# The output stores of every second pair of tiles, sent as 120 channels and 8 channels

## Chip, core and metric

The kernel runs on one core of a Trainium2 chip. The metric is the device time of one execution in microseconds; the kernel before takes 663.94 us (median of three runs, 661.92 to 664.46).

## What is computed

The input is one image of 256 channels and 96x96 points in float32. Two layers are added to it, one after the other. Only the second one matters here (b is 1, there are K = 4 heads):

```python
proj    = einsum('bchw,oc->bohw', gn(x), Wc) + bc
flows   = einsum('bchw,koc->kbohw', gn(x), Woff) + boff      # 4 offsets (x, y) for each point
weights = softmax(einsum('bchw,kc->bkhw', gn(x), Wwt) + bwt, axis=1)
feats   = bilinear sample of proj at (point + flow), zero outside the image, for each head
x       = x + einsum('kbohw,bkhw->bohw', feats, weights)
```

So each point of the output is a weighted sum of 16 vectors of 256 channels (4 heads x 4 corners), read at places that depend on the data.

## The kernel before

The image stays in SBUF as `xs` (128 channels on the partitions, two blocks `CB` of them, 9216 points). The points are cut into NT = 72 tiles of 128 points, and two tiles are a pair: 36 pairs.

The first 250 us or so load the image (SP queue), compute the first layer and write the result, turned so that one point is one row of 1 KB, into a `table` in HBM, each row twice: a row of the table holds the 256 channels of a point and of the point below it. Two neighbouring rows, 4 KB, hold all four corners of one sample.

The last 400 us or so are the second layer. For each tile and each head, GpSimd (POOL in the profile, line 948) issues one indirect DMA: 128 rows of 4 KB, 512 KB, one to a partition, into one of 16 places (`RING` = 4 tiles x 4 heads). The place can be refilled when both VectorE and TensorE have read it, so GpSimd waits on `added` and `used` before each issue. There are 72 x 4 = 288 of these gathers. Their destinations are called `v` and `stage` in the profile.

VectorE (DVE) sums 9 or 10 of the 16 corners of most tiles (lines 1155 and 1158, the first one of a tile at line 1155); TensorE (PE) sums the others as matmuls with diagonal matrices that ScalarE (ACT) makes (line 1528). VectorE joins the two sums (line 1165), TensorE turns the joined sum (line 1541) and multiplies it by the projection weights (lines 1553 and 1555), and VectorE adds the result of a pair to `xs` (line 1172), which raises `out_ready`. For the last pair the turn, the product and the addition go tile by tile (lines 1573, 1588, 1590 and 1203).

All stores of the output are on the SP queue. It waits for `out_ready` and issues one store for a pair: 128 partitions x 2 blocks x 256 points of float32, 256 KB in pieces of 1 KB (line 903), `LAST` = 35 times, and then one store of 128 KB for each of the last two tiles (line 908). SP has nothing else to do in the second layer. Nothing waits for a store but the end of the program, where SP waits for `written`.

A transfer is carried by the 16 DMA engines of the core together, and each engine that has done its part adds one to the transfer's semaphore; a wait for a multiple of 16 waits for all of them. The two kinds of transfer have different queues in the profile: q0 (software_dynamic) is what GpSimd issues, q1 (hardware_dynamic) what SP issues. q8 and q14 (instruction) are fetches of the program itself.

```python
for p in range(LAST):
    sp.wait_ge(out_ready, p + 1)
    sp.dma_start(out_c[:, :, p * 2 * P:(p + 1) * 2 * P], xs[:, :, p * 2 * P:(p + 1) * 2 * P]) \
        .then_inc(written, 16)
```

Of the kernel before, what the change touches and what calls it, by code (L numbers as in the profile page):

```python
# [34 lines left out]
P = 128  # L35
# [106 lines left out]
def build(nc, x, WqT, bq, WvT, bv, WpT, bp, out):  # L142
# [3 lines left out]
    out_c = out.rearrange("a (t p) h w -> p (a t) (h w)", p=P)  # L146
# [3 lines left out]
    with ExitStack() as ctx:  # L150
        def sb(name, shape, dt=F32):
            return ctx.enter_context(nc.sbuf_tensor(name, shape, dt))

        def sem(name):
            return ctx.enter_context(nc.semaphore(name))

        ps = ctx.enter_context(nc.psum_tensor("ps", [P, 8, CHUNK], F32))
        xs = sb("xs", [P, CB, HW])
# [22 lines left out]
        def column(name, n=1):  # L181
            if name not in col:
                col[name] = (sum(w for _, w in col.values()), n)
            a, w = col[name]
            return small[:, a:a + w]
# [13 lines left out]
        with ExitStack() as c0:  # L199
# [449 lines left out]
            with ExitStack() as c3:  # L649
# [16 lines left out]
                def chunk_of(n):  # L666
                    return n % 3 * ROUNDS + n // 3
# [60 lines left out]
                def sb3(name, shape, dt=F32):  # L728
                    return c3.enter_context(nc.sbuf_tensor(name, shape, dt))
# [6 lines left out]
                PAIRS = NT // 2  # L736
# [47 lines left out]
                share = sb3("share", [P, MOST])  # L784
                wy = sb3("wy", [P, 2, MOST, HEADS])

                DIAGS = 4
                assert max(NP) < 8

# [6 lines left out]
                RING = 4  # L796
                assert len(places) == DIAGS + RING * HEADS

                def place_of(t, k):
                    return DIAGS + t % RING * HEADS + k  # L800

# [9 lines left out]

                diag = [[a[:, n * P:(n + 1) * P] for n in range(max(NP))] for a in places[:DIAGS]]
                diag_sum = [a[:, 7 * P:8 * P] for a in places[:DIAGS]]

# [24 lines left out]
                weights_ready = sem("weights_ready")  # L839
                landed = {i: sem(f"landed{i}") for i in range(DIAGS, len(places))}  # L840
                added = sem("added")
# [8 lines left out]
                written = sem("written")  # L850
# [15 lines left out]
                def last_of_head(t, k):  # L866
                    return max(n for n, (head, _) in enumerate(ON_DVE[kind(t)]) if head == k)
# [5 lines left out]
                def used_by(t, k):  # L873

                    return t * HEADS + k + 1

                with nc.Block(no_gpsimd_drain=True) as block:
                    @block.sync
                    def _(sp):
                        sp.wait_ge(parts_ready, 2)  # L880
                        sp.dma_start(bias_row[:, :], bp.rearrange("(a n) -> a n", a=1).broadcast_to([P, NPROJ])).then_inc(grid_landed, 16)
                        sp.dma_start(grid[:, :, :], k_["grid"]).then_inc(grid_landed, 16)

                        sp.wait_ge(zeros_ready, 1)
                        sp.dma_start(table[0:W, 0:C], zeros).then_inc(edges_stored, 16)
                        sp.dma_start(table[HW:HW + W, C:2 * C], zeros).then_inc(edges_stored, 16)

                        def store(n):
                            u = n % SLOTS
                            for h in range(2):  # L890
                                sp.wait_ge(stage_ready, 2 * n + h + 1)
                                r = chunk_of(n) * CHUNK + h * 2 * P
                                sp.dma_start(table[r + W:r + W + 2 * P, 0:C].rearrange("(a p) c -> p a c", p=P),
                                             stage[u][h]).then_inc(stored[u], 16)
                                sp.dma_start(table[r:r + 2 * P, C:2 * C].rearrange("(a p) c -> p a c", p=P),
                                             stage[u][h]).then_inc(stored[u], 16)

                        for n in range(NCH):
                            store(n)

                        for p in range(LAST):
                            sp.wait_ge(out_ready, p + 1)
                            sp.dma_start(out_c[:, :, p * 2 * P:(p + 1) * 2 * P], xs[:, :, p * 2 * P:(p + 1) * 2 * P]) \
                                .then_inc(written, 16)
                        for i in range(2):
                            sp.wait_ge(out_ready, LAST + 1 + i)
                            here = slice((NT - 2 + i) * P, (NT - 1 + i) * P)
                            sp.dma_start(out_c[:, :, here], xs[:, :, here]).then_inc(written, 16)
                        sp.wait_ge(written, 16 * (PAIRS + 1))

                    @block.gpsimd
                    def _(pool):
# [294 lines left out]
                    def _(act):  # L1207
# [91 lines left out]
                        def diags(t):  # L1299
                            if t in FIRST:  # L1300
                                act.wait_ge(weights_ready, GROUP_OF[t] + 1)
                            if t >= DIAGS:
                                act.wait_ge(used, used_by(t - DIAGS, HEADS - 1))
# [376 lines left out]
```

## Time and profile before

| what | value |
|---|---|
| three runs, median (lowest to highest) | 663.94 us (661.92 to 664.46) |
| the profiled execution, its own time | 663.88 us |
| its span, first to last instruction | 661.9 us |
| mean granted clock of TensorE | 0.964 |
| busy: PE, DVE, POOL, ACT | 580.0, 550.2, 364.5, 362.3 us |
| moved by the DMA engines | 197.04 MB |

The span is what the profile's rows are placed in: a row at 640 us is 640 us after the first instruction. The device time of the same execution is 2.0 us more than the span. Packets are the pieces that DMA engines move; a queue's share is the time that its packets took, as a share of 16 engines over the stretch asked for. One engine that is busy all the time is therefore 1/16 or 6.25%.

### The profile page before, as it was taken

The page shows a single profiled execution, that of the slowest core. Times are in us where ns is not written, and L with a number is a line of the kernel's source. Part 1 is how long each engine was busy: PE and PEld are TensorE (multiplying, and loading weights), DVE is VectorE, ACT ScalarE, POOL GpSimd, SP SyncE. Part 2 cuts the span into 40 slices and gives each one's busy share as a digit, 9 for nine tenths or more (in the row PEclk, how much of TensorE's full clock was granted, in tenths as well). Part 3 has the DMA queues.
Part 4 walks back from the last instruction along what each step waited for, and adds up shares of the span by engine and source line. Part 5 has one row for each costly group of instructions (what it writes and reads, how often), then busy time and mean ns, then how long its engine had stood idle before and what let it go on. Part 6 is the DMA issues. An engine that isn't in the chain of part 4 may idle for free.

```text
span 661.9 us, 10746 instructions
## 1 busy us (share of the span) xinstructions
PE 580.0 (88%) x2992; PEld 457.2 (69%) x2992; DVE 550.2 (83%) x1316; ACT 362.3 (55%) x892; POOL 364.5 (55%) x385
## 2 busy tenths in 40 slices
PE   0589989999999789989969998989999899897987
PEld 0233477577888578878858996868777777675776
DVE  7899776458999878799888988978898879887886
ACT  0288876778888546165363556363645454535331
POOL 0040197115555447777776776776577566766620
PEclk9989999999999956799998999999999999999999
DMA  9910000214777778999999999999999999999982
GB/s 351 412 43 0 0 1 1 74 34 123 220 213 214 254 255 295 409 408 411 409 409 411 409 412 411 412 410 412 411 411 410 412 408 411 411 412 410 412 315 71
DMA packets 77367, 197.04 MB, mean 298 GB/s; under 512 B 7338, under 2 KB 36813, under 8 KB 77197
## 3 DMA queue, kind: packets, MB, share of 16 engines
q0 software_dynamic: 43488, 154.55, 59.4%
q1 hardware_dynamic: 33836, 42.03, 18.1%
q8 instruction: 14, 0.23, 0.2%
q14 instruction: 29, 0.23, 0.1%
HBM read 168.05 MB, written 28.51 MB: 297 GB/s over the span
## 4 chain that ended last, share of the span: by engine, by line
DMA 35%; PE 16%; issue 5%; DVE 4%; POOL 3%; ACT 1%; POOLq 0%; DVEq 0%
DMA v<-table,index 32%; PE ps L1528 9%; PE ps L1553 3%; DMA stage<-table,index 3%; DVE ps L1158 2%; POOL v L948 2%; PE ps L1555 2%; PE ps L1478 1%; POOL stage L948 1%; PE ps L1541 0%; DVE ps L1155 0%; ACT v L1305 0%; PE ps L1588 0%; POOL xs L935 0%; DVE wvs L1158 0%
## 5 line engine op out<-in xcount | busy, mean ns | idle before, releaser
L948 POOL DMA_INDIRECT v<-table,index x252 | 236.2, 937 | 106.6 <-DVE ps L1158 39.9
L1528 PE MATMUL ps<-v 128*128 128x256 f32 x786 | 205.8, 399 | 36.5 <-DMA v<-table,index 27.0
L1158 DVE SCALAR_TENSOR_TENSOR ps<-v,weights,ps 128x256 f32<-128x256 f32 x489 | 214.5, 483 | 1.5
L1528 PEld LDWEIGHTS ps<-v 128*128 128x128 f32 x786 | 142.3, 196 | 80.0 <-DMA v<-table,index 53.9
L1305 ACT ACTIVATE v<-ident,weights 128x128 f32<-128x128 f32 x464 | 139.4, 388 | 5.4 <-DVE wsum L1111 2.8
L935 POOL TENSOR_TENSOR xs<-xs,v 128x512 f32<-128x512 f32 x36 | 45.1, 1273 | 46.1 <-DVE v L1005 46.1
L1397 PE MATMUL ps<-wq,s_ring 128*128 128x256 f32 x288 | 68.1, 380 | 1.0 <-ACT ps L1241 0.9
L1318 ACT COPY pick_mask<-ps 128x512 f32<-128x512 f32 x18 | 10.5, 585 | 106.0 <-PE ps L1541 106.0
L1155 DVE TENSOR_SCALAR ps<-v,weights 128x256 f32<-128x256 f32 x72 | 34.9, 485 | 39.0 <-DMA v<-table,index 38.8
L1318 ACT COPY sample<-ps 128x512 f32<-128x512 f32 x17 | 9.9, 585 | 97.3 <-PE ps L1541 97.3
L1397 PEld LDWEIGHTS ps<-wq,s_ring 128*128 128x128 f32 x288 | 53.9, 191 | 9.4 <-issue 2.9
L559 PE MATMUL ps<-xs,wvs 128*128 (+1 forms) x104 | 49.9, 640 | 5.7 <-ACT v L494 3.4
L488 ACT ACTIVATE a_ring<-xs,small 128x768 f32<-128x768 f32 (+1 forms) x48 | 49.0, 1025 | 10.2 <-POOL t_ring L475 5.3
L475 POOL TENSOR_SCALAR t_ring<-a_ring,small 128x768 f32<-128x768 f32 x24 | 32.0, 1342 | 37.1 <-DVEq L416 34.9
L1555 PEld LDWEIGHTS ps<-v,bias 128*128 128x128 f32 x280 | 42.3, 191 | 3.6
L948 POOL DMA_INDIRECT stage<-table,index x36 | 33.7, 937 | 18.2 <-DVE ps L1158 10.9
L559 PEld LDWEIGHTS ps<-xs,wvs 128*128 128x128 f32 x104 | 20.4, 204 | 33.6 <-issue 25.9
L1555 PE MATMUL ps<-v,bias 128*128 128x128 f32 x280 | 42.5, 275 | 0.0
L1553 PE MATMUL ps<-pick_mask,wps 128*128 128x256 f32 x144 | 37.0, 380 | 0.0
L1528 PE MATMUL ps<-stage,v 128*128 128x256 f32 x142 | 34.6, 384 | 1.1 <-DMA stage<-table,index 0.9
L1553 PE MATMUL ps<-sample,wps 128*128 128x256 f32 x136 | 35.1, 381 | 0.0
L976 DVE TENSOR_REDUCE row_max<-ps 128x16 f32<-128x512 f32 x36 | 24.7, 687 | 10.0 <-PE ps L1397 9.0
(172 smaller groups left out, 926.8 us busy)
## 6 DMA issues: line engine op xcount, KB each, us to landing
table<-stage SPq DMA_DIRECT2D x72, 256.0 KB, 3.1
out_dram<-xs SPq DMA_DIRECT2D x35, 256.0 KB
xs<-in_x_dram SPq DMA_DIRECT2D x11, 768.0 KB, 11.3
v<-table,index POOLq DMA_INDIRECT x252, 16.0
early<-const_syn POOLq DMA_DIRECT2D x18, 192.0 KB, 3.6
ana<-const_ana SPq DMA_DIRECT2D x1, 2304.0 KB, 20.1
stage<-table,index POOLq DMA_INDIRECT x36, 15.7
xs<-in_x_dram SPq DMA_DIRECT2D x1, 512.0 KB, 14.8
```

The lines of the kernel that those rows point to most:

```text
L475: nc.gpsimd.tensor_scalar(t_ring[u][:, :], a_ring[u][:, :], column("less_mn")[:, t:t + 1], column("sc")[:, t:t + 1], ALU.add, ALU.mult).th ...
L488: S.activation(a_ring[u][:, :], xs[:, t, ds(j * (2 * QCH) + u * QCH, QCH)], ACT.Abs, scale=column("rstd")[:, t:t + 1], bias=column("nmr")[ ...
L559: m = T.matmul(ps[:, bank, :], wvs[:, kb, ob * P:(ob + 1) * P], xs[:, kb, ds(chunk * CHUNK, CHUNK)], start=kb == 0, stop=kb == CB - 1)
L935: nc.gpsimd.tensor_tensor(xs[:, cb, here], xs[:, cb, here], v[:, cb, here], ALU.add) \
L948: nc.gpsimd.indirect_dma_start(places[a], None, table, bass.IndirectOffsetOnAxis(ap=index[:, t, k:k + 1], axis=0)) \
L1155: V.tensor_scalar(to, corner, weight, None, ALU.mult).then_inc(added, 1)
L1158: V.scalar_tensor_tensor(to, corner, weight, ps[:, DVE_SUM, i * C:(i + 1) * C], ALU.mult, ALU.add).then_inc(added, 1)
L1305: S.activation(diag[t % DIAGS][n], ident[:, :], ACT.Copy, scale=weights[:, t, k, q:q + 1]) \
L1397: m = T.matmul(o, s2_ring[n % 2][kb][:, i * P:(i + 1) * P], wq[:, kb, :], start=False, stop=kb == CB - 1, skip_group_check=True)
L1528: m = T.matmul(ps[:, PE_SUM[i], 0:C], diag[2 * u + i][n], places[a][:, q * C:(q + 1) * C], start=n == 0, stop=n == len(mine) - 1)
L1553: T.matmul(o, wps[:, kb, cb * P:(cb + 1) * P], sample[u][:, kb, :], start=kb == 0, stop=False)
L1555: m = T.matmul(o[:, i * P:(i + 1) * P], bias[:, cb * P:(cb + 1) * P], diag_sum[2 * u + i], start=False, stop=i == 1)
```

## The change

The store of an even pair (p = 0, 2, ..., 34: 18 of them) becomes two transfers on the same queue, one of partitions 0 to 119 and one of partitions 120 to 127, each of both blocks and the same 256 points. Odd pairs and the last two tiles are stored as before. The last wait for `written` counts the 18 further transfers.

```diff
+                FEWER = (slice(0, 120), slice(120, P))
...
                         for p in range(LAST):
                             sp.wait_ge(out_ready, p + 1)
-                            sp.dma_start(out_c[:, :, p * 2 * P:(p + 1) * 2 * P], xs[:, :, p * 2 * P:(p + 1) * 2 * P]) \
-                                .then_inc(written, 16)
+                            here = slice(p * 2 * P, (p + 1) * 2 * P)
+                            for rows in (slice(0, P),) if p % 2 else FEWER:
+                                sp.dma_start(out_c[rows, :, here], xs[rows, :, here]).then_inc(written, 16)
...
-                        sp.wait_ge(written, 16 * (PAIRS + 1))
+                        sp.wait_ge(written, 16 * (PAIRS + 1 + (PAIRS // 2) * (len(FEWER) - 1)))
```

## Rows read from the trace of the kernel before

**Rows 1.** The page: DMA busy share and GB/s in 40 slices of 16.5 us.

```profile
DMA  9910000214777778999999999999999999999982
GB/s 351 412 43 0 0 1 1 74 34 123 220 213 214 254 255 295 409 408 411 409 409 411 409 412 411 412 410 412 411 411 410 412 408 411 411 412 410 412 315 71
```

**Rows 2.** The chain that ended last, 600 to 662 us (start, us, what).

```profile
591.01 18.17 DMA v<-table,index
...
612.43 17.12 DMA v<-table,index
...
632.78 18.46 DMA stage<-table,index
651.24 0.04 issue
651.28 1.13 PE ps L1528 x4
...
659.18 0.42 DVE xs L1203
```

**Rows 3.** Windows: us, PE, PEld, DVE, ACT, POOL busy (x instructions), PEclk, DMA share, GB/s.

```profile
450.00:500.00 50.00, 45.96 (x247) 37.98 (x246) 44.48 (x121) 24.99 (x78) 33.54 (x37) 1.00 1.03 411
638.00:639.00 1.00, 1.00 (x6) 0.88 (x5) 1.00 (x4) 0.00 (x0) 0.00 (x0) 1.00 1.05 406
643.00:644.00 1.00, 1.00 (x8) 0.81 (x6) 1.00 (x4) 0.57 (x2) 0.00 (x0) 1.00 0.11 42
644.00:645.00 1.00, 0.74 (x4) 0.30 (x2) 0.96 (x3) 0.60 (x3) 0.00 (x0) 1.00 0.06 26
648.00:649.00 1.00, 1.00 (x9) 0.95 (x8) 1.00 (x3) 0.00 (x0) 0.00 (x0) 1.00 0.06 25
650.00:651.00 1.00, 0.71 (x4) 0.28 (x2) 1.00 (x3) 1.00 (x5) 0.00 (x0) 1.00 0.06 23
651.00:652.00 1.00, 0.72 (x3) 0.67 (x4) 0.79 (x3) 0.20 (x1) 0.00 (x0) 1.00 0.01 2
```

**Rows 4.** Queue q0 in four windows: 640:641, 641:642, 642:643, 643:643.5.

```profile
q0 software_dynamic: 67, 0.23, 59.6%
...
q0 software_dynamic: 39, 0.13, 32.7%
...
q0 software_dynamic: 17, 0.06, 14.4%
...
q0 software_dynamic: 2, 0.01, 4.1%
```

**Rows 5.** DMA queues, 252 to 640 us: packets, MB, share of 16 engines.

```profile
q0 software_dynamic: 41242, 150.18, 96.6%
q1 hardware_dynamic: 8432, 8.13, 6.0%
q8 instruction: 7, 0.11, 0.1%
q14 instruction: 20, 0.16, 0.1%
```

**Rows 6.** Gathers (L948) from issue to landing, windows 300:340, 400:440, 600:640.

```profile
DMA to landing us min/median/max: 10.0/11.7/13.6
...
DMA to landing us min/median/max: 15.5/17.1/18.1
...
DMA to landing us min/median/max: 16.5/17.1/18.5
```

**Rows 7.** The page, costliest groups: busy, mean ns of one, idle before.

```profile
L948 POOL DMA_INDIRECT v<-table,index x252 | 236.2, 937 | 106.6 <-DVE ps L1158 39.9
L1528 PE MATMUL ps<-v 128*128 128x256 f32 x786 | 205.8, 399 | 36.5 <-DMA v<-table,index 27.0
L1155 DVE TENSOR_SCALAR ps<-v,weights 128x256 f32<-128x256 f32 x72 | 34.9, 485 | 39.0 <-DMA v<-table,index 38.8
```

**Rows 8.** The stores on SP's queue: ns of an issue (min/median/max), first and last start.

```profile
L903 SPq DMA_DIRECT2D out_dram<-xs x35: 372/372/378, 301.2 to 657.2; - x35
L908 SPq DMA_DIRECT2D out_dram<-xs x2: 373/422/470, 657.6 to 659.6; - x2
```

## Prediction

> **What bounds the kernel now.** I read the slices of the page first [rows 1]: from slice 16 on, about 260 us, the DMA engines move 408 to 413 GB/s without a break until the last two slices. Nothing in the second layer is as flat. The engines' waits say the same [rows 7]: VectorE stands idle 39.0 us ahead of the first corner of a tile, 38.8 of them for a gather, and TensorE 27.0 us of its 36.5 ahead of its corners for a gather. Between these waits they have room: VectorE is busy 44.48 of 50 us and TensorE 45.96 in a stretch of the middle, while the DMA share there is 1.03 [rows 3]. (It can exceed 1 because the durations of packets that follow each other on an engine overlap a little; I divide by 1.03 where it matters.) So the second layer goes at the pace of the DMA engines, and the gathers are 96.6 of their 102.8 percent, the stores 6.0 and the program's own fetches 0.2 [rows 5].
>
> Then I read the chain from its end [rows 2]. The last gather is issued at 632.78 us and lands at 651.24, 18.46 us later; what follows it takes 10.7 us to the end of the span. That latency is odd. After 639 us nothing more is issued, and 512 KB at 410 GB/s take 1.3 us. The fine windows show what happens [rows 3]: the share is 1.05 until 639 us, falls to 0.11 at 643 to 644, and from 644 to 651 us it stays at 0.06 with 23 to 26 GB/s, apart from one store. 0.06 is one engine of sixteen. Its last packets end at about 651.1 us, and the last gather lands then. Queue q0 alone [rows 4] gives the finish of the others: 59.6% of 16 engines at 640 to 641 us is 9.5 engines, then 5.2, then 2.3, and 4.1% at 643 to 643.5 is less than one. So fifteen engines have done their part of all gathers by about 643.0 us, on average by about 641, and **one engine ends 8.2 us after the second last** (651.24 - 643.0). A gather has landed only when all sixteen have done their part, so from 643 us on the program waits for that one engine.
>
> The delay was not there from the start. The latency of a gather is 10.0 to 13.6 us at 300 to 340 us, 15.5 to 18.1 at 400 to 440 and 16.5 to 18.5 at 600 to 640 [rows 6], while the share stays at 1.03: all engines always have work queued, so the late one costs nothing on the way, and its whole delay is paid once, at the end. The gathers deal equal parts to all, and so do the stores. What isn't dealt equally is the program's fetches, 7 on q8 and 20 on q14 [rows 5], and they may be the cause. No row gives the number of an engine, neither for a fetch nor for the late one.
>
> **The change part by part.** A store today: 8432 packets in 252 to 640 us are 31 stores of 272 packets, that is 16 pieces of 1 KB and one packet for the semaphore on each engine. Their share is 6.0% of 388 us, 23.3 us on each engine, 0.75 us a store, and divided by 1.03 it is **0.73 us of each engine's time for each store** [rows 5].
>
> *The transfer of 120 channels.* If its channels are dealt in equal whole parts, 15 engines take 8 channels each, as today, and one engine gets none. That engine saves 0.73 us for each even pair. The even pairs 0 to 30 are stored before the last gather's end: 16 stores, 16 x 0.73 = **11.7 us less on the engine left out**. The store of pair 32 comes at about 646 us, when its work would be over; pair 34 comes after everything. No row shows a transfer of 120 channels, so the price of its packets is bounded: from below 1 KB at today's price, from above twice that if the parts meet each other in reading SBUF, 0.73 us more on each of fifteen engines for each such store. I take today's price, because the pieces are of the same size and form.
>
> *The transfer of 8 channels.* One channel for each of eight engines, 1/8 of a store's part, 0.09 us each, 16 x 0.09 = **1.5 us more on these eight**. If it went over a single engine it would be 0.73 us on that one, the same as today if it were the one left out.
>
> *SP's queue.* 18 more issues at 0.372 us each [rows 8], 6.7 us in all, on an engine that does nothing else there and has 10 us between two pairs. Where it is tightest: the store of pair 34 is issued at 657.2, the next at 657.6 and the last at 659.6 us. One more issue moves the one of 657.6 by 0.37 us and leaves the last where it is. Cost 0; without that gap, 0.4 us. Nothing is queued behind these issues, and the final wait stands for the same bytes.
>
> *Compute engines.* Nothing is added for them. To end 7 us sooner they must keep a pace 7/390 or 2% higher; their waits for gathers (38.8 us on VectorE, 27.0 us on TensorE) are four to five times that. GpSimd issues a gather in 0.94 us and has 106.6 us of waits ahead of 252 of them [rows 7]. So the end follows the last landing.
>
> **The sum, if the late engine is the one left out.** It would finish at 651.2 - 11.7 = 639.5 us. The pace is then set by the second last of today, 643.0 us, or 644.5 us with its 1.5 us more. Between these I take 644.5, since eight of fifteen engines get that addition and several of them finish between 642 and 643 us. The last gather lands 651.2 - 644.5 = 6.7 us sooner, what follows is the same 10.7 us, and the profiled execution's 663.88 us become **657.2 us**. That execution is 0.06 us from the median of the runs, so the figure stands for both. Range of this case: 655.5 (nothing added to the second last, and half a microsecond of luck) to 660.5 (half the gain lost, in dearer packets or in a tail that doesn't follow).
>
> **A rule weighed against the rows.** The rows show that one engine is late and leave open which. The Trainium skill (DMA: Bandwidth & Descriptors, Queues, rings and completion order, under "How many engines (k)") states that such a transfer uses the largest number up to 16 that divides its slowest dimension, and from SP the lowest-numbered ones: 15 for 120 channels, 8 for 8 channels, so the last engine is left out. The same page (Latency and other measured facts) states that engines 7 and 15 are usually slower than the others. By the two together the late engine is 15, which gives the sum above, or 7, which gives the first rival. The trace has one late engine, not two.
>
> **The rivals.**
>
> *The late engine is one of the eight that get more.* It keeps its 11.7 us of stores and gets 1.5 us on top: the last landing goes from 651.2 to 652.7 us, the time to 665.4 us, +0.2%. For it: no row numbers the engine, and eight of sixteen would be such. Chance 0.17.
>
> *The late engine is neither.* Seven of sixteen take 8 channels in both forms. Nothing changes: 663.9 us. Chance 0.10. Of both together the change does what it says, but to an engine that nobody waits for.
>
> *Fewer engines than fifteen carry the 120 channels (the case on the other side).* The place is the deal of one transfer. If eight engines took 15 channels each, each would have 7/8 x 0.73 + 0.09 = 0.73 us more for an even pair, 11.7 us in all. If the late engine were among them, the last landing would be at 662.9 us and the time 675.6 us; if not, the second last would end at 643.0 + 11.7 = 654.7, 3.5 us after today's landing, and the time would be 667.4 us. It turns into a loss as soon as an engine other than the late one gets over 0.51 us more for each of the 16 stores (8.2/16). Against it: all transfers of today are of 128 or 96 channels and say nothing on 120. Chance 0.05, at 667 us, less for 675.
>
> *The delay goes but compute takes its place.* The last landing comes sooner and VectorE or TensorE is behind. For it: at 636 to 643 us TensorE is busy in nearly all of each microsecond. Against it: the waits of rows 7. It would leave about 1 to 3 us of the gain, 661 to 663 us. Chance 0.06.
>
> **How the numbers follow.** The forecast case gets what is left, 0.62. That the late engine is the one left out, and not one of the fifteen others, is my choice and no row's: taken blind it would be 1 in 16. The rows do say that a single engine is late, and that the 11.7 us taken from an engine exceed its 8.2 us, so that in this case the whole delay is removed. The predicted time is 657.2 us. Two in ten may be left out; above lie the 667 us case (0.05) and part of the 665.4 us one, below what is better than 655.3. The range is 655.3 to 665.3 us; the forecast case's own is 655.5 to 660.5. A difference of 0.5%, 3.3 us, is about what a measurement of this kernel can tell from no change. Faster by more than that: the forecast case, 0.62. Within: the first two rivals and the compute case, 0.33. Slower: 0.05.
>
> **What the profile after would show.** Queue q1 should have 18 more issues, of 240 and 16 KB. If the forecast holds, the fine windows have no stretch of several microseconds at a share of 0.06 ahead of the last landing; the share falls from 1.0 to 0 within 3 to 4 us; the latency of the last gathers is 11 to 13 us instead of 18; and the last landing is near 644.5 us. If the late engine isn't the one left out, the stretch at 0.06 is still there, 8 us long or 9.7. If fewer engines carry the 120 channels, several engines are late together and the share falls in steps from 0.5. If packets got dearer, the share of q1 for 31 pairs is well over 6.0% of 16 engines. The prediction is wrong above all if the late engine is another one than the last.

## The result, and the profile after

The changed kernel takes 665.35 us (median of 20 runs, 663.65 to 666.89) against 663.95 us (20 runs, 661.92 to 666.25): a ratio of 1.0022, 95% interval 1.0015 to 1.003. It is **1.4 us slower**, where 6.7 us faster was forecast. The first rival had 665.4 us.

The profiled execution has a span of 662.2 us. Its fine windows (us, busy time of PE, PEld, DVE, ACT and POOL with the number of instructions, PEclk, DMA share, GB/s), to be laid beside [rows 3]:

```profile
450.00:500.00 50.00, 45.95 (x246) 37.70 (x244) 44.38 (x121) 25.19 (x79) 33.70 (x36) 1.00 1.03 409
638.00:639.00 1.00, 1.00 (x6) 0.89 (x5) 1.00 (x4) 0.00 (x0) 0.00 (x0) 1.00 0.93 360
644.00:645.00 1.00, 0.98 (x5) 0.40 (x3) 0.96 (x4) 0.85 (x3) 0.00 (x0) 1.00 0.11 43
645.00:646.00 1.00, 0.11 (x1) 0.11 (x2) 1.00 (x3) 0.00 (x0) 0.00 (x0) 1.00 0.06 23
649.00:650.00 1.00, 1.00 (x9) 0.95 (x9) 1.00 (x4) 0.32 (x1) 0.00 (x0) 1.00 0.06 24
650.00:651.00 1.00, 0.94 (x5) 0.49 (x3) 1.00 (x4) 1.00 (x4) 0.00 (x0) 1.00 0.07 27
651.00:652.00 1.00, 0.48 (x2) 0.46 (x3) 0.83 (x2) 0.44 (x2) 0.00 (x0) 1.00 0.03 9
```

The stretch in which one engine of sixteen works alone, at 0.06, is still there, up to the last landing. What did change is its other end: at 638 to 639 us the share is 0.93 where it was 1.05, so an engine or two run out of work earlier. That fits a relief of an engine that nobody waits for. The last gather, in the chain that ended last (start, us, what), beside [rows 2]:

```profile
632.98 18.49 DMA stage<-table,index
651.47 0.04 issue
651.51 1.13 PE ps L1531 x4
...
659.41 0.42 DVE xs L1206
```

It lands at 651.47 us (651.24 before), 18.49 us after its issue, and the tail behind it is the same. Single executions of the kernel before lie some 4 us apart, so the 0.2 us between the two profiles is not the measure; the 1.4 us of the medians is.

Behind the late engine's last gather packet only stores are left, and only on this engine: the rest of the last one, of pair 32. The packets from there to 652 us, before (650.76:652) and after (650.992:652):

```profile
DMA packets 9, 0.01 MB, mean 7 GB/s; under 512 B 1, under 2 KB 9, under 8 KB 9
...
DMA packets 12, 0.01 MB, mean 10 GB/s; under 512 B 2, under 2 KB 12, under 8 KB 12
```

A packet under 512 B is one for a semaphore, so their number is the number of transfers that the engine carries. It was one and is two: the late engine carries the small transfer too.

The DMA queues in 252 to 640 us, beside [rows 5], and the issues of that stretch (KB each):

```profile
q0 software_dynamic: 41202, 150.02, 96.6%
q1 hardware_dynamic: 8544, 8.13, 6.0%
q8 instruction: 7, 0.11, 0.1%
q14 instruction: 20, 0.16, 0.1%
...
out_dram<-xs SPq DMA_DIRECT2D x16, 256.0 KB
...
out_dram<-xs SPq DMA_DIRECT2D x16, 240.0 KB
...
out_dram<-xs SPq DMA_DIRECT2D x16, 16.0 KB
```

The packets of q1 tell how many engines took part: a store has 256 pieces of 1 KB and one packet for the semaphore from each engine that carries it. 31 stores were 31 x 272 = 8432; now 15 whole ones are 15 x 272 and 16 divided ones 16 x 279, together 8544. (A sixteenth whole one is issued ahead of 640 us and moves behind it.) 279 is 256 + 23. If each transfer is dealt in equal whole parts, 23 can only be 15 + 8. So the 120 channels go over fifteen engines and the 8 channels over eight, as assumed. The share of 6.0% is unchanged to its last digit, so the pieces are hardly dearer.

### The profile page after: what moved, and what is told of

Read it like the earlier page. It is cut to its first block, busy times and chain, and to the rows that moved or that the text cites. A ratio compares the mean times of both kernels' runs of the same rounds, so it can differ in the third digit from the quotient of the medians.

```text
span 662.2 us, 10764 instructions
## 1 busy us (share of the span) xinstructions
PE 581.3 (88%) x2992; PEld 458.0 (69%) x2992; DVE 549.7 (83%) x1316; ACT 362.3 (55%) x892; POOL 364.4 (55%) x385
## 4 chain that ended last, share of the span: by engine, by line
DMA 33%; PE 18%; DVE 7%; issue 4%; POOL 2%; ACT 1%; DVEq 0%; POOLq 0%
DMA v<-table,index 29%; PE ps L1531 9%; DVE ps L1161 4%; DMA stage<-table,index 4%; PE ps L1556 3%; PE ps L1481 3%; PE ps L1558 2%; POOL v L951 1%; POOL stage L951 1%; DVE ps L1158 0%; PE ps L1544 0%; PE ps L1499 0%; PE ps L1591 0%; ACT v L1308 0%; PE ps L1433 0%
## 5 line engine op out<-in xcount | busy, mean ns | idle before, releaser
L1531 PE MATMUL ps<-v 128*128 128x256 f32 x786 | 208.1, 403 | 35.0 <-DMA v<-table,index 25.8
L1531 PEld LDWEIGHTS ps<-v 128*128 128x128 f32 x786 | 143.8, 198 | 79.0 <-DMA v<-table,index 53.4
```

What stands on the lines that cost most here:

```text
L1531: m = T.matmul(ps[:, PE_SUM[i], 0:C], diag[2 * u + i][n], places[a][:, q * C:(q + 1) * C], start=n == 0, stop=n == len(mine) - 1)
```

## The experiments

All are variants of the kernel before and are compared with it on the same chip. A difference given in us beside a ratio is the ratio times the time of the kernel before; the difference of the two medians shown can be up to 0.7 us away from it (e2 3.5, e3 3.4 and e4 3.0 us). Two theories stood at the start. A: the time is the sum of work of the one late engine up to the last landing, and that engine is one of the eight that get a further channel. B: it is the number of transfers that costs.

### More transfers, dealt alike

```diff
-sp.dma_start(out_c[:, :, here], xs[:, :, here]).then_inc(written, 16)
+for a, b in [(0, 128)] if p % 2 else [(0, 64), (64, 128)]:
+    sp.dma_start(out_c[a:b, :, here], xs[a:b, :, here]).then_inc(written, 16)
```

> The stores of every second pair in two transfers of 64 and 64 channels: 18 more transfers as in the change, but dealt to all sixteen engines alike (4 channels each, twice). Theory A (the change costs 1.4 us because its second transfer adds a channel to the one late engine): no engine carries more data than before, so 663.9 us, within 0.3. Theory B (it costs because there is one more transfer for each second pair, whoever carries it): the same loss as the change, 665.3 us.

Measured: 663.72 us against 663.45, ratio 0.9998 (0.9988 to 1.0008). 18 further transfers cost nothing that could be measured (0.5 us at most, by the interval) when all engines carry the same. B falls.

### The first eight engines, twice the dose

Here all 35 stores are divided. e2: `[(0, 120), (120, 128)]`. e3: `[(0, 112), (112, 120), (120, 128)]`. e4: `[(0, 112), (112, 119), (119, 126), (126, 128)]`.

> All 35 stores as 120 and 8 channels, twice the dose of the change. Theory A: the late engine gets 0.09 us more for each of about 32 stores ahead of the last landing, 2.9 us, so 666.8 us. Theory B: twice the loss of the change, the same 666.8 us. If the late engine carries none of the 8 channels (theory C) and the loss of the change was something else, 663.9 to 665.4 us.

Measured: 666.93 us, ratio 1.0042 (1.0028 to 1.0057), +2.8 us (1.9 to 3.8 by the interval): twice the change's 1.4.

> All 35 stores as 112, 8 and 8 channels: if 112 channels are dealt to all sixteen engines (7 each) and 8 to eight engines, the first eight carry 9 and the others 7 instead of 8. Theory A (late engine among the eight): one channel more for about 32 stores, +2.9 us, 666.8 us. Theory C (late engine among the other eight): one channel less, -2.9 us, 661.0 us. Theory B (each further transfer costs about 1.4/16 us): 64 further transfers, about +5.6 us, 669.5 us.

Measured: 666.86 us, ratio 1.0041 (1.0026 to 1.0055), +2.7 us, and not the 5.6 us of theory B. The last eight engines lose a channel here, the first eight gain one, and the kernel is slower: the late engine is among the first eight (theory C, that it is one of the others, asked for a gain). In the chain of this kernel the last gather lands 3.2 us later than in [rows 2]:

```profile
635.79 18.67 DMA stage<-table,index
654.46 0.04 issue
```

> All 35 stores as 112, 7, 7 and 2 channels: seven engines carry the two transfers of 7, two of them the last one as well, and nine engines carry 7 channels instead of 8. If the late engine is the eighth in the order in which transfers are dealt (theory A7), it loses one channel for about 32 stores, -2.9 us, and its stretch at a share of 0.06 ahead of the last landing shrinks by as much: 661.0 us. If it is one of the first seven (theory A0 to 6), +2.9 us or, for the first two, +5.8 us: 666.8 to 669.7 us. Theory B: the most transfers of all, the slowest of the four, about +8 us.

Measured: 666.46 us, ratio 1.0032 (1.0021 to 1.0044), +2.1 us. The eighth engine would have given a gain: it isn't the eighth. The first two get two channels more instead of one, which would have been about twice the loss of e3; so it is one of the third to the seventh. The packets behind its last gather packet (654.044:655) say so without the price: three transfers, those of 112, 7 and 7 channels, and not the one of 2.

```profile
DMA packets 11, 0.01 MB, mean 9 GB/s; under 512 B 3, under 2 KB 11, under 8 KB 11
```

In e3 and in e4 there are 8928 packets of q1 in 252 to 640 us, 31 x (256 + 16 + 16): 8 + 8 and 7 + 7 + 2 engines carry the small transfers.

### Which engine

Stores of even pairs only, the odd ones whole. e5 and e9: `[(0, 112), (112, 116), (116, 120), (120, 124), (124, 128)]`. e6 and e10: `[(0, 112), (112, 117), (117, 122), (122, 127), (127, 128)]`.

> Stores of every second pair as 112, 4, 4, 4 and 4 channels, the others whole: the first four engines carry 11 channels of such a store, the others 7 instead of 8. The runs so far put the late engine among the third to the seventh in the order of dealing. If it is the fifth, sixth or seventh, it loses one channel for 16 stores, -1.5 us (662.2 us, ratio 0.998), unless one of the first four, with 4.4 us more, becomes the last. If it is the third or fourth, +4.4 us (668.1 us, ratio 1.007).

> Stores of every second pair as 112, 5, 5, 5 and 1 channels: the first engine carries 11 channels of such a store, the next four 10, the others 7 instead of 8. Late engine sixth or seventh: -1.5 us, ratio 0.998. Late engine third, fourth or fifth: +2.9 us, 666.6 us, ratio 1.0045. Together with the run with four this tells the fifth from its neighbours.

Measured: 709.28 us, ratio 0.9984 (0.9954 to 1.0013), and 712.54 us, ratio 1.001 (0.9982 to 1.0038), beside 711.69 us of the kernel before on this chip. Neither answers the question. All runs of this set, the kernel before among them, took over 706 us; what differs in the trace is the rate of the gathers, mostly 340 to 390 GB/s and uneven. I call this the low rate. Both kernels were measured again at the usual one.

> The kernel of e5_first4 once more, because all runs of that call, the kernel before among them, took 707 to 716 us with the DMA engines at 340 to 390 GB/s instead of 411. The stores of every second pair as 112, 4, 4, 4 and 4 channels. Late engine fifth to seventh in the order of dealing: -1.5 us, ratio 0.998. Third or fourth: +4.4 us, ratio 1.007.

Measured: 666.66 us against 663.77, ratio 1.005 (1.0036 to 1.0065), +3.3 us. The late engine is one of the first four.

> The kernel of e6_first5 once more: stores of every second pair as 112, 5, 5, 5 and 1 channels. Late engine sixth or seventh: -1.5 us, ratio 0.998. Third to fifth: +2.9 us, ratio 1.0045.

Measured: 665.54 us, ratio 1.003 (1.0018 to 1.0042), +2.0 us. The two intervals overlap (2.4 to 4.3 and 1.2 to 2.8 us), so the times alone do not tell two channels more from three. The packets of the late engine behind its last gather do (e9, 653.681:655, and e10, 653.803:655):

```profile
DMA packets 19, 0.01 MB, mean 11 GB/s; under 512 B 5, under 2 KB 19, under 8 KB 19
...
DMA packets 16, 0.01 MB, mean 10 GB/s; under 512 B 4, under 2 KB 16, under 8 KB 16
```

In e9 it carries all four transfers of 4 channels, so it is one of the first four. In e10 it carries the three of 5 and not the one of 1, so it is not the first. With e4 only the third and the fourth are left. Then the first three against the fourth (e13 and e17), even pairs as `(0, 112)`, five times 3 channels and 1 channel:

> Stores of every second pair as 112, five times 3 and 1 channels, the others whole: the first engine carries 13 channels of such a store, the second and third 12, the others 7 instead of 8. If the late engine is the third: four channels more for 16 stores at the 0.06 to 0.07 us each that the runs with four and five measured, +4.2 us, ratio 1.006. If it is the fourth: one channel less, -1.1 to -1.5 us, ratio 0.998, unless the first engine, with 5.4 us more, becomes the last.

Measured, at the low rate: 717.65 us against 715.67, ratio 1.0035 (1.0008 to 1.0062). The sign would point to the third engine; it is not used, because at this rate no engine works alone for long (shown with e15 below).

> The kernel of e13_first3 once more. Late engine third: four channels more for 16 stores, +4.2 us, ratio 1.006. Late engine fourth: one channel less, ratio 0.998.

Measured: 663.38 us against 664.19, ratio 0.999 (0.9971 to 1.0008). The time alone excludes the loss of the third, 1.006, and is not clear of no change. The windows of this run say more:

```profile
647.00:648.00 1.00, 1.00 (x10) 0.95 (x9) 1.00 (x4) 0.00 (x0) 0.00 (x0) 1.00 0.27 108
648.00:649.00 1.00, 1.00 (x8) 0.92 (x7) 1.00 (x4) 0.60 (x2) 0.00 (x0) 1.00 0.19 75
649.00:650.00 1.00, 0.66 (x4) 0.23 (x2) 1.00 (x4) 1.00 (x4) 0.00 (x0) 1.00 0.19 72
650.00:651.00 1.00, 0.57 (x3) 0.52 (x4) 0.79 (x3) 0.15 (x1) 0.00 (x0) 1.00 0.05 16
```

A share of 0.25 is four engines, 0.19 three. Engines that got four or five channels more have come up to the late one, and the last gather lands at 650.38 us. The packets of the trace from 648 us on form three unbroken sequences, one to an engine. Two end with at least five small transfers each, 2 pieces and a semaphore packet; the third has 14 pieces, the part of the 112 channels, and no small transfer. This third one is the late engine, since all other engines are done by 643 us in the kernel before and get less here. So it is none of the first three, and by e9 it is one of the first four: **the fourth in the order of dealing**. This takes for granted that transfers of n channels always go to the first n engines, which the packets of e3, e4, e9, e10 and e17 all agree with, and that the same engine is late on the three chips used.

### Why one engine is late

e7 and e11 add instructions to VectorE's program, e8 and e12 the same to ScalarE's.

```diff
                             for a in TURNS[2 * p + 1]:
                                 add(*a)
+                            for _ in range(14):
+                                dve.sem_inc(pad, 1)
                             join(2 * p)
```

> Adds 14 semaphore increments that nothing waits for to VectorE's program in each pair, 504 in all; no other work. Theory F (the late engine is the one that fetches VectorE's program, and each fetch of 8 KB puts it back by about 1 us): 504 instructions are four further fetches on q14, so the stretch in which one engine works alone ahead of the last landing grows by about 4 us, and the time to about 668 us. Theory G (one engine is late for another reason): the stretch stays 7 to 8 us; the time grows only if the increments themselves hold VectorE up.

> The same 504 increments in ScalarE's program. Theory F: four further fetches on q14, but on another DMA engine, which ends some 7 us or more ahead of the late one: no change, 663.7 us. If all fetches of q14 went over the late engine: about 4 us more, as with VectorE. Theory G: no change.

Measured, at the low rate: 716.26 us, ratio 1.0064 (1.0037 to 1.0091), and 711.69 us, ratio 1.0014 (0.998 to 1.0048). The sign is as in theory F, but here the chain runs over VectorE for 25% of the span, so the loss may have another way. The repeats:

> The kernel of e7_pad_dve once more: 504 semaphore increments more in VectorE's program. Theory F (the late engine fetches VectorE's program, about 1 us for each 8 KB): the stretch of one engine alone ahead of the last landing grows from 7 to about 11 us and the time by about 4 us, to 667.5 us. Theory G (late for another reason): the stretch stays; a slower kernel would then show waits of the other engines for VectorE.

> The kernel of e8_pad_act once more: the same 504 increments in ScalarE's program. Theory F: 663.7 us, the stretch stays at 7 to 8 us, since ScalarE's fetches put back another engine. If all fetches of q14 went over the late engine: +4 us.

Measured: VectorE's 668.31 us, ratio 1.006 (1.0046 to 1.0074), +4.0 us; ScalarE's 664.06 us, ratio 1.0003 (0.9992 to 1.0014). In 252 to 640 us q14 has 23 fetches with VectorE's and 24 with ScalarE's instructions, against 20 [rows 5], about the same number more in both. The windows with VectorE's:

```profile
640.00:641.00 1.00, 1.00 (x8) 0.95 (x7) 1.00 (x4) 0.00 (x0) 0.00 (x0) 1.00 1.01 414
643.00:644.00 1.00, 1.00 (x6) 0.87 (x6) 1.00 (x3) 0.00 (x0) 0.00 (x0) 1.00 0.06 25
651.00:652.00 1.00, 1.00 (x10) 0.79 (x8) 0.85 (x4) 0.26 (x1) 0.00 (x0) 1.00 0.07 27
653.00:654.00 1.00, 0.70 (x2) 0.30 (x2) 0.90 (x3) 0.50 (x2) 0.00 (x0) 1.00 0.06 26
654.00:655.00 1.00, 0.20 (x1) 0.20 (x2) 0.18 (x1) 0.00 (x0) 0.00 (x0) 1.00 0.04 14
```

The others finish by 643 us as before, and the one works alone until 654.8 us, where the last gather lands, 3.6 us later than in [rows 2]. With ScalarE's instructions the windows from 648 to 651 us are at 0.07, 0.06 and 0.06, and at 651 to 652 us at 0.01, as in [rows 3]. So fetches of VectorE's program put back the engine that is late, about 1 us for each 8 KB, and those of ScalarE's don't.

One of these fetches falls into the stretch of e11 in which the engine works alone on the gathers, and there its price can be seen. Queue q0 in 647:648, then q0 and q14 in 649.47:650.79:

```profile
q0 software_dynamic: 6, 0.02, 5.1%
...
q0 software_dynamic: 2, 0.01, 4.2%
q14 instruction: 1, 0.01, 1.5%
```

Ahead of the fetch a 4 KB packet of a gather takes 0.16 us. The fetch takes 0.31 us, and the two gather packets behind it take 0.50 and 0.39 us, the store piece between them 0.16 instead of 0.05; the engine loses 0.95 us in all. The same figure, a fetch of about 0.33 us with two packets of about 0.49 us directly behind it, stands ten times in the trace of the kernel before from 297 us to the end, each time with a loss of 0.96 to 0.98 us where the engines are all busy, and fourteen times in e11 (two fetches meet at 314 us and count as one). It stands ten times in e12 too: the fetches that the padding of ScalarE added take 0.31 to 0.32 us and have no slow packets behind them. Four more such losses are 3.9 us, and the landing moved by 3.6. Ten of them are 9.8 us, an estimate from these packets, and the late engine ends 10 us after the mean of the others (651 and about 641 us). So these fetches account for its whole delay, as near as this sum can tell. Why the packets behind them are slow, and only behind VectorE's, is open.

### Work moved behind the last landing

The stores from pair 23 on wait for the last gather (e15 and e18, shown below). In e14 the number 10 in this line is 6, in e16 it is 13.

```diff
                         for p in range(LAST):
+                            if p == LAST - 2 - 10:
+                                sp.wait_ge(landed[place_of(NT - 1, HEADS - 1)], 16 * use_of(NT - 1))
                             sp.wait_ge(out_ready, p + 1)
```

> Stores as before, but those of pairs 27 to 32 are issued only when the last gather has landed. Theory A (the late engine's sum of work ahead of the last landing sets the time): it has six stores less ahead of it, 6 x 0.73 = 4.4 us, so 659.3 us. They fit behind the landing: 4.4 us of work in the 10.7 us of the tail. Rival (the DMA engines as a whole or the compute engines set the end, and one late engine is a symptom): little or nothing, 662 to 664 us.

> Stores of pairs 23 to 32 deferred until the last gather has landed. Theory A: 10 x 0.73 = 7.3 us off the late engine, 656.5 us, with 7.3 us of stores in a tail of 10.7 us. If the compute engines become the bound, 658 to 661 us.

> Stores of pairs 20 to 32 deferred. Theory A for the landing: 9.5 us sooner. But now 9.5 us of stores and 2 us of latency stand behind it, as long as the tail of 10.7 us, and the last store queues behind them: no better than with ten, 656 to 658 us.

Measured, again at the low rate, beside 715.67 us: 716.19 us, ratio 1.0005 (0.9981 to 1.003); 715.72 us, ratio 0.9987 (0.9962 to 1.0013); 716.92 us, ratio 1.0007 (0.9985 to 1.0028). No dose does anything there. The windows of the run with ten (e15):

```profile
692.00:694.00 2.00, 2.00 (x11) 1.77 (x10) 2.00 (x6) 0.00 (x0) 0.27 (x1) 1.00 1.02 375
694.00:696.00 2.00, 2.00 (x13) 1.79 (x12) 2.00 (x6) 0.00 (x0) 0.00 (x0) 1.00 0.74 289
696.00:698.00 2.00, 2.00 (x16) 1.87 (x15) 2.00 (x6) 0.02 (x1) 0.00 (x0) 1.00 0.04 16
```

Between the full share and nearly none lie 2 to 3 us: no engine works alone for long. The deferral is not the reason, since e13, which defers nothing, goes from a share of 0.97 at 693 to 694 us to 0.03 at 697 to 698. Nor is the landing what counts most at this rate: 19.1 us of the span of e15 lie behind the last gather packet, where it was 11.2 us. So theory A has no hold there. What lowers the rate was not found out.

> The kernel of e15_defer10 once more, stores of pairs 23 to 32 issued when the last gather has landed. Theory A (the late engine's work ahead of the last landing sets the time): 10 x 0.73 = 7.3 us off it, 656.5 us. If compute becomes the bound, 658 to 661 us. Rival (one late engine is a symptom): 662 to 664 us.

Measured: 658.37 us against 664.19, ratio 0.9906 (0.9883 to 0.9929), **5.8 us faster than the kernel before by the medians, 6.2 by the ratio, and about 7 us faster than the changed one**. That is 1.9 us over theory A's figure and inside the range given for the compute engines as the bound, so the time alone does not decide between them; the trace does. Its windows, and SP's queue (start, us from the first to the last of the group):

```profile
641.00:642.00 1.00, 1.00 (x8) 0.92 (x7) 1.00 (x4) 0.00 (x0) 0.00 (x0) 1.00 0.06 25
644.00:645.00 1.00, 0.97 (x5) 0.52 (x4) 0.90 (x3) 0.89 (x4) 0.00 (x0) 1.00 0.00 0
648.00:649.00 1.00, 1.00 (x9) 0.96 (x8) 0.85 (x2) 0.00 (x0) 0.00 (x0) 1.00 1.02 343
654.00:655.00 1.00, 0.00 (x0) 0.00 (x0) 0.00 (x0) 0.00 (x0) 0.00 (x0) 1.00 1.03 317
655.00:656.00 1.00, 0.00 (x0) 0.00 (x0) 0.00 (x0) 0.00 (x0) 0.00 (x0) 1.00 0.48 134
...
644.40 8.05 SPq L905 DMA_DIRECT2D out_dram<-xs  x12
652.49 1.49 SPq L910 DMA_DIRECT2D out_dram<-xs  x2
```

The last gather has landed by 644.40 us, 6.8 us sooner than in [rows 2], close to the 7.3 us worked out. The late engine is as late as before, the stretch at 0.06 has only moved. Behind the landing the stores now keep all engines at 1.03 from 646 to 655 us, while the last addition is over by 653.1 us (the window from 654 us has no compute at all): the tail is 12.0 us where it was 10.7, and takes 1.3 us back. With fewer stores deferred it might be a little better; that ran only at the low rate.

## Why the prediction was wrong

**The step that failed** is the choice in the sum, "if the late engine is the one left out", given 0.62. The rows did not number the engine, the text said so, and blind it would have been 1 in 16. e3, e4, e9, e10 and e17 put it fourth in the order of dealing, twelve places from the one left out, and in the changed kernel it carries the transfer of 8 channels: 1.4 us more where 11.7 us less were forecast. The chance should have followed the rows: with eight of sixteen engines in the group that gets more, the first rival was the likeliest by count alone. The Trainium skill (DMA: Bandwidth & Descriptors, Latency and other measured facts) has engines 7 and 15 as usually the slower ones; by these runs it is neither, and the measurement decides. The rule of the Trainium skill on the number of engines (the same page, Why a DMA increments its semaphore by 16 and not by 1, under "How many engines (k)") agrees: 15 and 8, by the count of 8544 packets.

**The price of what did happen was right.** 16 stores x 0.09 us on the late engine were 1.5 us, the rival's time 665.4 us; measured +1.4 us (1.0 to 2.0) and 665.35. That the two times agree to 0.05 us is luck; the interval is wider. Doubled, +2.8 (e2) and +2.7 us (e3). With the other divisions a channel seems to cost less, 2.1/32 = 0.07 us in e4, 2.0/32 = 0.06 in e10 and 3.3/48 = 0.07 in e9, but 0.09 us lies at the upper end of these intervals, so a difference isn't shown.

**What bounds the kernel** was read rightly: one engine ends last and the program waits for it. e18 takes 10 stores from it, 7.3 us of work, and the landing comes 6.8 us sooner; e11 gives it fetches, and it is 3.6 us later. The cause that the prediction left as a possibility, the program's fetches, is shown for VectorE's, by adding to them and by the packets behind each; taking them away was not tried. Two readings were loose and change nothing: "several" engines finishing between 642 and 643 us are one or two besides the late one (14.4% of 16 engines is 2.3 with it), and the late engine's last packets at 651.1 us are a store's, its last gather packet ends at 650.77.

**SP's queue at no cost** held: e1 has 18 further transfers and no measurable loss. **No dearer packets** held: 6.0% as before.

**The rivals.** That fewer engines than fifteen carry the 120 channels is refuted by the count. That compute would take the place of the delay could not show in the changed kernel; in e18 the compute engines followed by almost all of the 6.8 us (the last addition ends 6.5 us sooner), and what is missing of the rest in the span is the stores'.

## What to carry to other kernels

When a transfer has landed only once all sixteen engines have done their part, look in fine windows at how the DMA share falls ahead of the last landing: a long step at 1/16 is one engine's sum of work, and in such a kernel only work taken from that engine, or moved behind the landing, comes back. Moving work between engines needs to know which one it is; a probe that gives one group of engines a little more and another a little less tells that in a few runs, before anything is forecast on it. Where one engine works alone at the end, the number of its semaphore packets tells which transfers reach it, and does so more sharply than the times. Work that can wait, such as stores, is better put into the idle tail, up to what the tail holds.

## What the runs showed that was not expected

Fetching VectorE's program costs one DMA engine about 1 us for each 8 KB while all are busy (3.6 us for four more fetches in e11): a third of it is the fetch itself, two thirds are two slow packets behind it. The fetches must nearly all go over the same engine, since their losses add up on it. 504 instructions of no work made the kernel 4.0 us slower with VectorE still having idle time, and the same 504 on ScalarE 0.2 us, within the error. And the same program ran at 664 us in most sets of runs and at 712 and 716 us in two, where the gathers moved mostly 340 to 390 GB/s instead of 411 and no effect of one late engine was seen. It is no fixed property of a chip: the chip of e5 to e8, at 712 us, is by its number in the record the one that ran e17 and e18, beside 664 us, half an hour later.
